# Second attention of a two-layer transformer kernel: its loop written out, its gathers of expert outputs spread over eight steps

## The reference

```python
x = x + _L0_xattn_ref(_layernorm(x), ctx_1024, ctx_1024, ...)
x = x + _L0_ffn_ref(_layernorm(x), ...)      # top 2 of 8 experts for each token
x = x + _L1_xattn_ref(_layernorm(x), ctx_1024, ctx_1024, mask, ...)   # causal
x = x + _L1_ffn_ref(_layernorm(x), ...)
# in _L1_xattn_ref:
Q, K, V = proj(query, Wq, Nq), proj(key, Wk, Nk), proj(value, Wv, Nk)
scores = jnp.einsum('bhqd,bhkd->bhqk', Q, K) / np.sqrt(D_KEY)
attn = jax.nn.softmax(jnp.where(causal | masked, NEG_INF, scores), axis=-1)
return jnp.einsum('bhqk,bhkd->bhqd', attn, V) @ Wo
```

## Time and profile before

| | |
|---|---|
| median of 3 runs | 412.98 us (412.91 to 413.5) |
| the profiled execution | 414.6 us, its span 412.9 us |
| busy over the span | TensorE 79%, VectorE 67%, ScalarE 52%, GpSimd 42% |
| steps 1 to 9 of the second attention | 251.57 to 329.26 us |

### The profile page before, as it was taken

The page is one execution under the profiler, slowest core; times in us unless marked ns, Lnnn a source line. Parts: engine busy times, 40 slices in busy tenths (PEclk is TensorE's granted clock), DMA queues, the critical chain, the costliest instruction groups (busy, mean ns, idle before and its releaser), DMA issues. The chain is left out here.

```text
span 412.9 us, 10070 instructions
## 1 busy us (share of the span) xinstructions
PE 324.2 (79%) x3320; PEld 244.6 (59%) x3322; DVE 277.7 (67%) x838; ACT 214.1 (52%) x442; POOL 173.6 (42%) x295
## 2 busy tenths in 40 slices
PE   1684778898977999999989876584888899747564
PEld 0352666777766677777687844463566667524442
DVE  6765667888845664346562465966697889557994
ACT  2252356677671774333547523441455466757884
POOL 7335051143526154441324748664354464611432
PEclk9988589999996999999999998987799999986999
DMA  7555964444258000015568423223162332000111
GB/s 210 142 151 115 241 172 121 135 146 134 61 140 291 1 27 25 21 44 116 129 175 239 132 69 99 80 70 75 48 159 83 95 118 60 4 2 0 28 32 44
DMA packets 62871, 41.64 MB, mean 101 GB/s; under 512 B 39192, under 2 KB 53488, under 8 KB 62832
## 3 DMA queue, kind: packets, MB, share of 16 engines
q1 hardware_dynamic: 53360, 36.35, 31.5%
q10 hardware_dynamic: 8448, 2.69, 2.6%
q0 software_dynamic: 1024, 2.10, 1.8%
HBM read 27.16 MB, written 13.50 MB: 98 GB/s over the span
## 5 line engine op out<-in xcount | busy, mean ns | idle before, releaser
L1111 ACT ACTIVATE probs<-ps_e 128x512 f32<-128x512 f32 x128 | 76.1, 595 | 59.4 <-PE ps_e L918 58.6
L999 DVE TENSOR_REDUCE neg<-ps_s 128x4 f32<-128x512 f32 x128 | 86.2, 685 | 29.6 <-PE ps_s L901 27.7
L901 PE MATMUL ps_s<-k_rows,q_rows 96*128 96x128 bf16 x512 | 54.1, 233 | 7.5 <-PEq L473 3.9
L918 PE MATMUL ps_e<-q_rows,k_rows 128*128 128x128 bf16 x512 | 51.9, 228 | 5.8 <-DMA q_rows<-neg_t 5.0
L901 PEld LDWEIGHTS ps_s<-k_rows,q_rows 96*128 96x128 bf16 x512 | 40.0, 104 | 21.0 <-issue 9.1
L918 PEld LDWEIGHTS ps_e<-q_rows,k_rows 128*128 128x128 bf16 x512 | 36.8, 102 | 9.8 <-DMA q_rows<-neg_t 6.3
L932 PE MATMUL ps_pv<-probs,v_aug 128*32 128x128 f32 x1024 | 37.6, 288 | 3.2 <-POOL probs L1184 3.1
L1518 DVE SCALAR_TENSOR_TENSOR x_all<-ps_ym,comb,x_all 128x128 f32<-128x128 f32 x64 | 17.9, 344 | 31.2 <-PE ps_ym L1631 31.2
L1761 ACT ACTIVATE hid<-ps_h,w 128x512 f32<-128x512 f32 x32 | 21.9, 687 | 31.5 <-PE ps_h L1621 31.4
L897 PE MATMUL ps_s<-upper,identb 128*128 128x512 bf16 x64 | 25.5, 398 | 15.2 <-DVE neg L999 10.1
L1631 PEld LDWEIGHTS ps_ym<-w,hid 128*128 128x128 f32 x256 | 30.3, 192 | 3.4 <-issue 3.3
(11 more groups left out here) (244 smaller groups left out, 705.8 us busy)
## 6 DMA issues: line engine op xcount, KB each, us to landing
k_rows<-k_dram SPq DMA_DIRECT2D x32, 144.0 KB
q_rows<-q_dram SPq DMA_DIRECT2D x32, 144.0 KB
k_rows<-k_dram SPq DMA_DIRECT2D x16, 288.0 KB
q_rows<-q_dram SPq DMA_DIRECT2D x16, 288.0 KB
k_dram<-parts SPq DMA_DIRECT2D x35, 128.0 KB, 2.4
q_dram<-parts SPq DMA_DIRECT2D x18, 128.0 KB, 2.2
w<-in_w SPq DMA_DIRECT2D x8, 257.0 KB, 4.5
xs_dram<-zero SPq DMA_DIRECT2D x1, 1472.0 KB, 9.6
```

The lines of the kernel that those rows point to most:

```text
L901: last = pe.matmul(ps_s[:, q % 2, j * P:(j + 1) * P], q_rows[0:ROW_MAX, r, h, :], k_rows[0:ROW_MAX, r, h, :], start=(layer == 0), stop=Tru ...
L918: last = pe.matmul(ps_e[:, q % 2, j * P:(j + 1) * P], k_rows[:, r, h, :], q_rows[:, r, h, :], start=not masked, stop=True, skip_group_chec ...
L999: dve.tensor_reduce(neg[:, s, q * HQ:(q + 1) * HQ], ps_s[:, q % 2, :].rearrange("p (h k) -> p h k", h=HQ), AX_X, ALU.max, negate=True).the ...
L1111: act.activation(probs[:, s, q, :], ps_e[:, q % 2, :], ACT.Exp, scale=SCALE).then_inc(exp_done, 1)
```

## The change

The loop of the second attention is written out in all steps (the first attention keeps its loop), so that `after` can name steps in it. On VectorE a list of pieces takes the place of the single one. The gathers of the sorted groups come in pairs (one batch, two DMAs) behind the steps -1 to 4, apart from four behind step -3. The additions and the query chain of group 2 are one step later than before, those of group 3 three steps later, on all engines; the stores are behind `load(7)` and `load(11)`, where they were behind `load(6)` and `load(8)`.

```diff
-PROJECTED = {2: 2, 4: 3}
+PROJECTED = {3: 2, 7: 3}
...
-            with eng.Fori(1, (B - 4) // SLOTS) as i:
+
+            def four(i):
                 for j in range(SLOTS):
                     if beside:
                         beside(j, i - 1)
                     step(i * SLOTS + (2 + j), (2 + j) % SLOTS)
+                    if isinstance(i, int) and i * SLOTS + 2 + j in after:
+                        after[i * SLOTS + 2 + j]()
                 if behind:
                     behind(i - 1)
+
+            if layer == 0:
+                with eng.Fori(1, (B - 4) // SLOTS) as i:
+                    four(i)
+            else:
+                for i in range(1, (B - 4) // SLOTS):
+                    four(i)
...
-                    if b in (6, 8):
-                        queries.store(sp, {6: 2, 8: 3}[b])
+                    if b in (7, 11):
+                        queries.store(sp, {7: 2, 11: 3}[b])
...
-                    if piece and layer == 1:
-                        piece[0](q)
+                    if layer == 1:
+                        for do in piece:
+                            do(q)
...
-                piece[:] = [do]
+                piece.append(do)
...
-            run(dve, step, {0: lambda: query_pieces((2, 0)), 1: lambda: query_pieces((2, 1)),
-                            2: lambda: query_pieces((2, 2), (3, 0)), 3: lambda: query_pieces((3, 1)),
-                            4: lambda: query_pieces((3, 2))} if also else {}, beside)
+            run(dve, step, {1: lambda: query_pieces((2, 0)), 2: lambda: query_pieces((2, 1)),
+                            3: lambda: query_pieces((2, 2)), 5: lambda: query_pieces((3, 0)),
+                            6: lambda: query_pieces((3, 1)), 7: lambda: query_pieces((3, 2))} if also else {}, beside)
...
             run(pool, step, {-3: lambda: gather(2, (0, 1)),
-                             -2: lambda: gather(2, (2,)),
-                             -1: lambda: gather(2, (3,)),
-                             0: lambda: gather(3, (0,)),
-                             1: lambda: (queries.root(pool, 2), gather(3, (1,))),
-                             2: lambda: (queries.leave(pool, 2), gather(3, (2, 3))),
-                             3: lambda: queries.root(pool, 3),
-                             4: lambda: queries.leave(pool, 3)} if also else {1: add_bias}, beside)
+                             -1: lambda: gather(2, (2,)),
+                             0: lambda: gather(2, (3,)),
+                             1: lambda: gather(3, (0,)),
+                             2: lambda: (queries.root(pool, 2), gather(3, (1,))),
+                             3: lambda: (queries.leave(pool, 2), gather(3, (2,))),
+                             4: lambda: gather(3, (3,)),
+                             6: lambda: queries.root(pool, 3),
+                             7: lambda: queries.leave(pool, 3)} if also else {1: add_bias}, beside)
```

## The result

The changed kernel takes 415.55 us (median of 11 runs, 412.48 to 417.64), the kernel before, run beside it, 412.98 (11 runs, 409.34 to 414.14). The ratio is 1.0077, with a 95% interval of 1.0049 to 1.0105: slower by 0.8%, where 407.6 had been forecast. The ratios leave out slower executions (more than 1.5% above the fastest of their kernel), so a ratio can differ a little from the quotient of two medians. The profiled execution after took 415.81 us, its span is 414.1.

What follows compares the result with a forecast made beforehand. No engine was full; gather waits lengthened steps 1 and 3, and row loads bounded plain steps. Long pairs 46.4 to 35.4 us, plain steps 31.3 to 37.1, loop 0.2: 5.4 us saved, forecast 407.6, range 403.4 to 411.0.

Steps and rivals of the forecast that it cites:

- S times: TensorE's starts of steps, at batch b + 2's first scores; forecast S2 258.5, S4 276.1, S6 291.2, S8 308.95, S10 324.05.
- Gathers: Fewer gathers ahead of batch 0's clearing, the rest issued earlier relative to the additions; VectorE's `yg` waits below 1 us in all.
- Step 1: S1 to S2: now a plain step, ended by load(4) issued at 251.81; 6.9 us long.
- Steps 2 and 3: S2 to S4: group 2's additions and projection, additions from 259.9, then 16.2 us carried over from the old order; S4 = 276.1.
- Steps 4 and 5: S4 to S6: plain, but load(8) waits for group 2's store; 8.7 for the store plus 6.4 for the load, 15.1 us.
- hand-overs: Group 2's store to load(8), group 3's to load(12), each load waiting for the store directly ahead; 15.1 us against 12.5 plain.
- Steps 6 and 7: S6 to S8: group 3's additions and projection, 1.2 + 15.45, plus 1.1 us for the inputs' variance pieces beside the additions.
- Steps 8 and 9: S8 to S10: repeat of steps 4 and 5 with load(12) behind group 3's store; 15.1 us, S10 = 324.05.
- The loop: Second attention's loop written out: branch and register-computed waits go; gain 0.2 us, bounds 0 and 1.
- The rest of the kernel does not change: Everything outside S1 to S10 was taken to keep its time, so only that stretch of 77.7 us was rebuilt.
- The one that was slower: Laying of batch 6's and 10's maxima lands 4.3 us after the rows, stopping TensorE twice, 8.6 us: 416.2; chance 0.07.
- No change: Gathers' waits in steps 1 and 3 only hid another VectorE limit; the pairs keep about 41 us; chance 0.04.

Runs made afterwards that it cites:

- the clearings cut: Changed kernel with GpSimd's causal clearing covering 128 x 4 instead of 128 x 512: 402.39 us, 0.9790 of before; the kernel before with the same cut: 406.53 us.
- the split moved: Changed kernel with the split of the sorted groups' queries moved from the first to the second quarter of steps 4 and 8: 413.13 us, 1.0038 of before.
- after without the hand-over: Changed kernel whose loads of batches 8 to 15 read batches 4 to 7's queries, waiting for no store of groups 2 and 3: 416.02 us, 1.0049 of before.
- group 2 as before: Changed kernel with group 2's gathers, additions, chain and store as before the change, group 3's as changed: 412.98 us, 1.0029 of before.
- the run with two clearings: Changed kernel with two GpSimd clearings per batch instead of three, the third quarter masked by a matmul: 411.84 us, 1.0006 of before.

## Why the prediction was wrong

The working is followed by its S times; the two numbers are those of the two profiles of after.

**Gathers.** Right: no wait for `yg` is left. **Step 1.** 6.9 forecast, 5.6 and 6.3 measured. That load(4) ends it held in the second profile only (TensorE waited 1.66 us for it). The time won here brought nothing: VectorE began group 2's additions at 259.96 and 260.08 in the two, where 259.9 had been forecast. That is luck. The working put a reduction alone between S2 and the additions, and VectorE had the split of the maxima and the last output's division to do as well.

**Steps 2 and 3.** 17.6 forecast, 21.1 and 19.2 measured. This is the first step that failed: "The same work, root, projection and all, stands here in the same order". From the first addition to S4 it took 18.2 us in both profiles, where 16.2 had been carried over. GpSimd's order beside it was the same (root, two gathers, fill, clearings), but VectorE's was not: two instructions stood ahead of the normalisation that were not there before, since the pipeline had been one step younger then, a batch's residual addition and its statistics. They put it 0.55 us further back against GpSimd's row. Before, it began 1.31 us ahead of the fill (268.57) and was done as the fill began; after, it began 0.78 us ahead of the fill (270.33) and ended 0.09 us behind the first clearing (271.55). VectorE's timeline before, and after:

```profile
267.26 1.33 DVE L212 TENSOR_SCALAR q_xn<-x_all,q_mean,q_rstd 128x128 f32<-128x128 f32 x4
...
269.55 2.09 DVE L212 TENSOR_SCALAR q_xn<-x_all,q_mean,q_rstd 128x128 f32<-128x128 f32 x4
```

Then TensorE's granted clock fell. From the normalisation's end to the next step, with 31 or 32 matmuls each, in the first and second profile of before and the first of after:

```profile
268.59:273.98 5.39, 5.25 (x32) 3.96 (x33) 1.67 (x4) 1.88 (x4) 2.67 (x7) 0.68 0.05 12
...
269.04:272.77 3.73, 3.58 (x31) 2.68 (x32) 1.56 (x5) 1.87 (x4) 2.67 (x7) 1.00 0.07 18
...
271.64:278.15 6.51, 6.37 (x31) 4.44 (x32) 1.74 (x4) 2.06 (x4) 1.43 (x4) 0.55 0.01 3
```

The second profile of after has 6.47 us at 0.55. So the first profile of before, from which the working took its 16.2, held 1.7 us more than the second in this stretch, at the lower clock, and after has another 1.1; ahead of this stretch TensorE had waited 1.42 us for the normalisation in both profiles of before and 2.37 in both of after. With the clearings cut, step 3 is 9.11 us instead of 13.00, at a clock of 1.00 instead of 0.74.

**Steps 4 and 5.** 15.1 forecast, 16.2 and 16.3 measured. The store was issued 7.2 us into step 4, where 4.6 was forecast, because of the split's 3.03 us. "Steps 4 and 5 are plain" held only without the held instruction: then the two hand-overs measured 15.03 and 15.27. The load after the store took 5.4 us, of 6.4 forecast. The working's other estimate, 3.6 us for two loads of 288 KB, comes to 3.4 if its own terms are added up, and the section that it cites in the Trainium skill ("DMA: Bandwidth & Descriptors", section "Anatomy of one DMA") gives them for DMAs that GpSimd issues, where these are SyncE's; the 5.4 us lie above both.

**Steps 6 and 7.** 17.75 forecast, 19.3 and 19.2 measured: mis-sized by 1.5 us. The first pass of additions was not held (1.13 us), the second was (2.16, second profile of after), and so was the normalisation (1.82, where group 3's had 1.57 in both profiles of before). TensorE ran both steps at clocks of 0.78 and 0.85, and it entered step 6 after the wait of 2.18 us. How the 1.5 us divide between these was not tried.

**Steps 8 and 9.** 15.1 forecast, 14.9 measured twice. The size is right, not the reason: TensorE waited for no load at S10, though the store had been issued 4.8 us into step 8 as forecast: step 8 was 8.16 us long for VectorE (7.99 us busy) by itself. So this size is luck. **The loop.** 0.2 forecast; no difference could be measured.

**"The rest of the kernel does not change"** failed too. Behind S10 there are 1.7 to 2.7 us more, depending on the two profiles compared. In the first two it is 2.0: 0.7 by S13, in which TensorE waited 0.55 and 0.74 us for two loads, and 1.3 from S13 to the end, which begins with the stretch of the lower clock.

The sum closes in the first profile: S10 came 4.4 us later than forecast (-1.4 + 3.5 + 1.1 + 1.5 - 0.2, rounded), 2.0 came behind it and 0.2 of the loop stayed out, which makes 409.2 + 6.6 = 415.8. On top of that the profile of before lay 1.6 us above its median and that of after 0.3, so that the working started from an execution of before that was longer than usual.

**The rivals.** The one that was slower named the laying of the maxima as its mechanism. No such wait appeared. That its 416.2 lies 0.7 us from the measured median is luck. "No change", with VectorE as the hidden limit, was the nearest in mechanism and had 0.04. It missed that VectorE's work is no constant: the earlier trace rows were read as 7.3 and 8.5 us of work in steps 1 and 3, though these were the work *beside the gathers as they stood*.

**Is the cause settled?** Shown: without most of the clearings the changed order is the faster one (402.4 against 406.5), the place of two gathers is worth 4 us, and the hand-over is worth about 3 us once uncovered. The Trainium skill ("SBUF — State Buffer", section "SBUF: two separate sides") says that VectorE and GpSimd share a port pair as an exclusive lock, taken for a whole instruction, when VectorE has two SBUF inputs (then only against a GpSimd instruction that reads SBUF) or runs in a two-port mode. The rows agree: the split has two inputs in SBUF, fill and clearings read SBUF, and the maxima, which read PSUM, took 0.67 to 0.69 us in all 64 places of the second attention. By the rule a waiting instruction would lose one GpSimd instruction's time, though, 0.6 us here; the trace shows it wait out a fill and three clearings. Argued only: that the 2.6 us by which after is slower are made of these pieces; no run adds them up. Open: what brings the lower clock in steps 3 and 6 and behind S13, which no run held apart and which is worth up to 2.7 us in step 3 alone (6.5 us at 0.55 against 3.73 at 1.00).

## What to carry to other kernels

When an edit takes work off one engine's program (gathers here), ask which instructions of *other* engines then fall beside each other that did not before; a queue that is full of DMA issues can be the cover of a VectorE instruction. Read an instruction's price in the row where it stands, and again beside each neighbour that it may get: 0.69 and 3.03 us are the same instruction. If two limits lie in one step, removing one alone can show far less than it is worth (1.2 us for the hand-over, and 3 with the split moved), so take each out with the other one already out; and profile the kernel before twice before building a sum of tenths on one execution.

## What was unexpected of the hardware

A 128 x 512 subtraction on VectorE with both inputs in SBUF took 0.69 us beside indirect gathers issued by GpSimd, and 3.03 us, in each of four profiles of kernels that put it there (after twice, after without the hand-over, group 2 as before), beside a fill and three clearings of 0.62 us each; with two clearings 2.29, with clearings of 128 x 4 0.82. With full clearings it did not get in between GpSimd's instructions, which follow each other closely; with the small ones it did, and GpSimd waited. Nor is the outcome fixed for one place: a cast of 128 x 16 in step 2 took 0.17 to 0.20 us where nothing held it, but beside two clearings it once got in between them (0.41 us) and once waited both out (1.15 us), in the first and the second profile of after:

```profile
257.47 0.41 DVE L1016 CAST neg_parts<-neg 128x16 bf16<-128x16 f32 x1
...
257.38 1.15 DVE L1016 CAST neg_parts<-neg 128x16 bf16<-128x16 f32 x1
```

One single store landed 4.6 us after its issue in the run with two clearings (2.0 to 2.8 us in both profiles of after), and TensorE waited 4.52 us for `load(8)` there: the landing of a store scatters more than the 3.3 us that the prediction allowed.
